# A batch's key-times-value product: from two products beside the running sums to one in an expert slot's bank, copied by ScalarE and masked by GpSimd

## The chip, the cores and the metric

The kernel runs on one NeuronCore of a Trainium2 chip. The metric is the device time of one execution in microseconds, lower is better. The profiled execution is one run with the hardware profiler on; its span goes from the first to the last instruction.

## The reference

Two layers over x of 16 batches of 256 tokens of 128 channels (4096 tokens). All of it is float32.

```
xn = layernorm(x)
x  = x + attn0(xn) + moe(xn)          # causal linear attention, 16 heads of 8; top 2 of 8 experts
xn = layernorm(x)
x  = x + attn1(xn) + channel_mix(xn)  # linear attention over 512 tokens; gated square of relu
```

attn0 is the part at issue. Keys and queries are rotated and put through elu + 1; then, for each batch and head,

```
KV_t    = sum of k_s (x) v_s for s <= t       # 8 x 8, running over the tokens
K_sum_t = sum of k_s for s <= t
y_t     = (q_t KV_t) / max(q_t K_sum_t, 1e-6)
```

The mixture of experts takes each token's two best of eight experts, with hidden = gelu(x W1 + b1), out = hidden W2 + b2, weighted by the two gates.

## The kernel before

**Tiles.** A tile is 128 tokens, a batch is two tiles. The experts' work is laid out in 71 slots of 128 rows, each with one expert. GpSimd gathers a slot's rows from a copy of xn in HBM by an indirect DMA (`gather`, L503), six slots ahead, into a ring of four buffers. TensorE transposes the rows (`xg_transpose`, L559), multiplies by W1 (`up`, L575), ScalarE copies and applies gelu (L596, L604), TensorE multiplies by W2 (`down`, L587), ScalarE copies the result out (L614) and SP stores it. From slot 17 on GpSimd also gathers experts' results back (`gather_y`, L520), five for six slots.

**Attention between the slots.** `steps` (L883) lays one tile of attention beside about every second slot: SUMS_AT is 1, 3, 5 and so on, 66 for the last. For tile i = 2b + r the vector engine multiplies keys by values (`attn_outer`, L685: 9 x 16 x 8 columns, the ninth of 9 being the keys themselves, put there by ScalarE at L671), ScalarE rounds that to a high part (L696), the vector engine takes the low part as a difference (L703; for tiles 1 to 12 GpSimd does a third of it, L716), and TensorE sums both over the tokens by a triangular matrix in three banks (`attn_cumsum`, L783 and L784). The vector engine multiplies the sums by the queries (`attn_apply`, L795) and reduces (L806); after the second tile come a reciprocal (L812), a division (L820) and phi (L656), which is elu + 1 for the batch after the next.

**What the first tile gives to the second.** Tile 1 of a batch also needs all of tile 0's sums. They come as a product of their own: K^T V of the first tile (`attn_KV`, L729, 128 columns, and L730, 16 columns of ones for the sum of keys), written by TensorE right ahead of the running sums of the batch before into the gap behind the first bank's 384 columns; the banks' windows therefore stand 520 columns apart (`NEXT`). The vector engine multiplies by the heads' mask into SBUF (`attn_mask_KV`, L735, tile KV0). Beside an expert slot TensorE then transposes the second tile's queries (L748, at slots QT_AT) and multiplies them by KV0 (L753, at slots REST_AT = SUMS_AT[2b]; batch 0 at slot 2), both written into columns 128 and up of the slot's own bank, between `up` and `down`; ScalarE copies them out ahead of the slot's result (`attn_beside_scalar`, L757 and L762).

**Order.** It is written out by hand. Each engine runs its own list in order and waits on semaphores. TensorE takes, in a step j: transpose of slot j+2, `up` of j+1, running sums if j is in SUMS_AT, what stands beside the slot, `down` of j. ScalarE takes copy of j+2, gelu of j+1, keys and high part in the step behind a sum, and the copies of slot j. A float32 product shows as two records in the trace.

**Gates.** The experts' gates are worked out by the vector engine ahead of the slots (`gates`, L1837 to L1843), and split in two parts (`split_gates`, L1849 and L1850); TensorE first needs them at the transposes of batch 0, in step 6.

## Time and profile before

| | |
|---|---|
| time, three runs | 348.57, 349.37, 349.54 us; median 349.37 us |
| profiled execution | 349.86 us, span 348.1 us |
| TensorE (PE) busy | 330.2 us, 95% |
| VectorE (DVE) busy | 318.9 us, 92% |
| ScalarE (ACT) busy | 278.4 us, 80% |
| GpSimd (POOL) busy | 225.3 us, 65% |
| granted TensorE clock | 0.995 of full |
| slots | 62 to 264 us of the span |

A row of the time line gives start, duration, engine, line, operation, tile written and tiles read, shape, and in brackets how long the engine had been idle before it and what ended that. A duration runs a little past the start of the next instruction, since instructions are pipelined, so that start to start is the pace. A wait for several semaphores is put down to the one that came last by the profile.

### The profile page before, as it was taken

To read this page: it belongs to the slowest core of one execution; us is meant where nothing else is said; L and a number is where in the kernel's file an instruction comes from. 1 tells how busy PE (TensorE), PEld (TensorE's weight loads), DVE (VectorE), ACT (ScalarE), POOL (GpSimd) and SP (SyncE) were. 2 spreads that over 40 slices of the span, in tenths; PEclk is the share of its full clock that TensorE was granted. 3 is DMA by queue.
4 is the path that set the end of the run, shared out by engine and by line. 5 is a ranking of instruction groups with operands and counts; after the bars stand their busy time and mean duration, and the time that the engine had idled before them with its cause. 6 is when DMAs were issued, how large, how long until landed. Compare 5 with 4: busy or idle time off the path is not lost.

```text
span 348.1 us, 9108 instructions
## 1 busy us (share of the span) xinstructions
PE 330.2 (95%) x2457; PEld 293.9 (84%) x2457; DVE 318.9 (92%) x590; ACT 278.4 (80%) x805; POOL 225.3 (65%) x238
## 2 busy tenths in 40 slices
PE   7999968889999999999999899999998999999995
PEld 3878424689999999999999899999997788778875
DVE  5899999989999999999899899999979799998665
ACT  2987956977899898889788778879997788777751
POOL 3799101876776688777777768777877278874110
PEclk9999989999999999999999999999999999999999
DMA  5785595334444555664655555676452002221012
GB/s 161 213 237 141 147 427 206 107 109 137 137 138 138 140 149 162 159 189 136 178 164 161 166 161 153 160 190 161 122 144 70 1 17 54 59 57 32 30 32 60
DMA packets 47120, 47.04 MB, mean 135 GB/s; under 512 B 8528, under 2 KB 35312, under 8 KB 46816
## 3 DMA queue, kind: packets, MB, share of 16 engines
q1 hardware_dynamic: 42032, 37.23, 35.4%
q0 software_dynamic: 4320, 8.86, 10.8%
q10 hardware_dynamic: 720, 0.38, 0.5%
q8 instruction: 22, 0.36, 0.4%
q14 instruction: 26, 0.21, 0.2%
HBM read 32.88 MB, written 13.50 MB: 133 GB/s over the span
## 4 chain that ended last, share of the span: by engine, by line
PE 78%; DVE 15%; DMA 2%; issue 2%; ACTq 1%; ACT 0%; SPq 0%; DVEq 0%
PE banks L575 17%; PE banks L587 17%; PE banks L783 5%; PE banks L784 5%; PE banks L1106 3%; PE banks L559 2%; PE banks L1182 2%; PE banks L1135 2%; PE banks L1164 2%; PE banks L1144 2%; PE banks L868 2%; PE banks L1116 2%; PE banks L1152 2%; DVE qk_exp L408 2%; PE banks L1171 2%
## 5 line engine op out<-in xcount | busy, mean ns | idle before, releaser
L503 POOL DMA_INDIRECT xg<-xn_rows,slot_tok x71 | 85.6, 1206 | 44.7 <-DVE slot_at L1819 23.0
L604 ACT ACTIVATE xT<-banks,b1T 128x128 f32<-128x128 f32 x284 | 81.8, 378 | 12.3 <-PE banks L575 11.9
L520 POOL DMA_INDIRECT qk_exp<-expert_rows,ranki x64 | 70.2, 1097 | 18.4 <-issue 17.1
L575 PE MATMUL banks<-xgT,w 128*128 128x128 f32 x568 | 75.5, 276 | 0.2 <-ACT xgT L596 0.2
L587 PE MATMUL banks<-w_sb,xT 128*128 x568 | 75.2, 275 | 0.1
L587 PEld LDWEIGHTS banks<-w_sb,xT 128*128 128x128 f32 x568 | 69.3, 192 | 0.9 <-issue 0.3
L575 PEld LDWEIGHTS banks<-xgT,w 128*128 128x128 f32 x568 | 69.0, 192 | 0.8 <-issue 0.7
L795 DVE TENSOR_TENSOR cq<-banks,phi 128x1152 f32<-128x1152 f32 x32 | 43.2, 1350 | 5.7 <-PE banks L784 5.7
L806 DVE TENSOR_REDUCE late<-cq 128x144 f32<-128x1152 f32 (+1 forms) x32 | 45.5, 1421 | 0.1
L696 ACT CAST high<-outer 128x1152 fp32r<-128x1152 f32 x32 | 37.0, 1156 | 6.8 <-DVE outer L685 5.0
L703 DVE TENSOR_TENSOR low<-outer,high 128x1152 fp32r<-128x1152 f32 (+1 forms) x32 | 38.7, 1210 | 1.5 <-ACT high L696 1.3
L685 DVE TENSOR_TENSOR outer<-phi,qkv 128x1024 f32<-128x1024 f32 x32 | 39.4, 1233 | 0.0
L783 PE MATMUL banks<-high,tri_r 128*128 128x384 f32 x96 | 34.8, 363 | 0.0
L784 PE MATMUL banks<-low,tri_r 128*128 128x384 f32 x96 | 32.2, 336 | 0.0
L335 PE MATMUL banks<-zeros_bf 128*128 128x512 bf16 x96 | 26.3, 415 | 1.0 <-DVE zeros_bf L1660 1.0
L321 ACT ACTIVATE xn_all<-x_sb,shift,rstd 128x128 f32<-128x128 f32 x60 | 24.9, 487 | 0.0
L1057 POOL TENSOR_TENSOR outer<-outer,x_sb 128x512 f32<-128x512 f32 x7 | 8.9, 1276 | 22.4 <-DVE outer L1052 22.3
L614 ACT COPY ye<-banks 128x128 f32<-128x128 f32 x71 | 19.9, 280 | 2.3 <-PE banks L587 2.3
L559 PE MATMUL banks<-cst,xg 128*128 128x128 f32 x71 | 19.6, 276 | 2.1 <-issue 1.9
L716 POOL TENSOR_TENSOR low<-outer,high 128x384 fp32r<-128x384 f32 x12 | 12.8, 1070 | 10.9 <-DVE phi L656 8.0
L596 ACT COPY xgT<-banks 128x128 f32<-128x128 f32 x71 | 19.6, 276 | 0.0
L303 POOL TENSOR_TENSOR rstd<-ve,mhalf 128x4 f32<-128x4 f32 x16 | 18.5, 1154 | 1.2
(224 smaller groups left out, 701.3 us busy)
## 6 DMA issues: line engine op xcount, KB each, us to landing
w<-in_L_ffn_W SPq DMA_DIRECT2D x71, 256.0 KB
expert_rows<-ye SPq DMA_DIRECT2D x71, 64.0 KB
expert_rows<-x_sb SPq DMA_DIRECT2D x2, 2048.0 KB, 9.8
x_sb<-in_L_attn_x SPq DMA_DIRECT2D x8, 256.0 KB, 4.5
xn_rows<-xn_all SPq DMA_DIRECT2D x8, 256.0 KB, 4.1
w_sb<-in_L_ffn_W SPq DMA_DIRECT2D x8, 256.0 KB, 4.5
out<-outer SPq DMA_DIRECT2D x7, 256.0 KB, 2.3
xg<-xn_rows,slot_tok POOLq DMA_INDIRECT x71
```

The lines of the kernel that those rows point to most:

```text
L503: pool.indirect_dma_start(out=xg[n][:, :], out_offset=None, in_=xn_dram, in_offset=bass.IndirectOffsetOnAxis(ap=slot_tok[:, j:j + 1], axis ...
L520: pool.indirect_dma_start(out=y_moe[:, i, k, :], out_offset=None, in_=y_dram, in_offset=bass.IndirectOffsetOnAxis(ap=ranki[:, 0, k, i:i + ...
L575: last = nc.tensor.matmul(slot_bank(j)[:, c * P:(c + 1) * P], w1[n][:, c * P:(c + 1) * P], xgT[p][:, :], start=True, stop=True)
L587: last = nc.tensor.matmul(y, hidT[p][:, c, :], w2_sb[:, ds(e * NC + c, 1), :], start=(c == 0), stop=(c == NC - 1))
L604: last = nc.scalar.activation(hidT[p][:, c, :], slot_bank(j)[:, c * P:(c + 1) * P], ACT.Gelu_apprx_tanh, bias=b1T[:, ds(e * NC + c, 1)])
L685: nc.vector.tensor_tensor(outer_of(r)[:, 0:DH, :, :], k.unsqueeze(1).broadcast_to([P, DH, H, DH]), vv.unsqueeze(3).broadcast_to([P, DH, H, ...
L696: nc.scalar.copy(high[kept(r, p)], outer[r]).then_inc(high_ready, 1)
L703: nc.vector.tensor_tensor(low[n][:, cols], outer[r][:, cols], high[n].bitcast(f32)[:, cols], ALU.subtract).then_inc(low_ready, 1)
L783: nc.tensor.matmul(o, tri_r[:, :], high[at][:, cols], start=True, stop=False)
L784: last = nc.tensor.matmul(o, tri_r[:, :], low[at][:, cols], start=False, stop=True)
L795: nc.vector.tensor_tensor(cq.rearrange("p (n e h d) -> p n e h d", n=NBANK, h=H, d=DK)[:, :, :, :, 0:DH], cum.rearrange("p n (e h d) -> p ...
L806: nc.vector.tensor_reduce(sums[:, r, :, :].rearrange("p h e -> p e h"), cq4[:, :, :, 0:DK if r else DH], AX.X, ALU.add).then_inc(sums_read ...
```

## The change

It does five things.

1. The product of keys and values is one matmul of 144 columns, its ones taken from sixteen columns behind the values (which held the router's logits), set to one by a GpSimd memset once the logits are read. It stands in `attn_beside`, in columns 368 to 511 of the slot's bank, at slots KV_AT = 0 for batch 0 and SUMS_AT[2b-2] + 1 for the others.
2. ScalarE copies it to KV0 in that slot's `attn_beside_scalar`; GpSimd multiplies KV0 by the mask in place, at the head of the next iteration of its loop over slots, ahead of a gather.
3. The running sums have no product ahead of them, don't wait for KV_ready, and their banks' windows stand 512 columns apart.
4. The vector engine no longer has the mask in its list.
5. Of the gates' operations the last three come after the first low part (`share_gates`), and `split_gates` comes after tile 0.

Some semaphores are merged, which moves no work. The diff, cut to its core:

```
-    def attn_KV(pe, b):
-        pe.wait_ge(phi_ready, b + 1)
-        k = phib[b % 2][:, 0, D:2 * D]
-        nc.tensor.matmul(first_sums[:, 0:D], k, qkv3[:, 2 * b, 2 * D:3 * D], start=True, stop=True)
-        nc.tensor.matmul(first_sums[:, D:DA], k, ones_r[:, 0:H].bitcast(f32), start=True, stop=True).then_inc(KV_ps, 1)
-    def attn_mask_KV(v, b):
-        v.wait_ge(KV_ps, b + 1)
-        nc.vector.tensor_tensor(KV0..., first_sums..., const("head_mask")..., ALU.mult).then_inc(KV_ready, 1)
+    def attn_mask_KV(pool, b):
+        pool.wait_ge(KV_raw, b + 1)
+        kv0 = KV0.rearrange("p (e h) -> p e h", h=H)
+        nc.gpsimd.tensor_tensor(kv0, kv0, const("head_mask")..., ALU.mult).then_inc(KV_ready, 1)
+    KV_AT = [0] + [SUMS_AT[2 * b - 2] + 1 for b in range(1, B)]
...
     def attn_beside(pe, j, bank):
+        if j in KV_AT:
+            b = KV_AT.index(j)
+            pe.wait_ge(phi_ready, b + 1)
+            if b == 0:
+                pe.wait_ge(pool_const, 5)
+            nc.tensor.matmul(bank[:, 4 * D - DA:4 * D], phib[b % 2][:, 0, D:2 * D], qkv3[:, 2 * b, 2 * D:2 * D + DA],
+                             start=True, stop=True)
...
     def attn_beside_scalar(act, j, bank):
+        if j in KV_AT:
+            nc.scalar.copy(KV0, bank[:, 4 * D - DA:4 * D]).then_inc(KV_raw, 1)
...
     def attn_cumsum(pe, b, r, p):
-        if i >= 1:
-            pe.wait_ge(KV_ready, 1 + i // 2)
-        if i == 0:
-            attn_KV(pe, 0)
-        if r == 1 and till(b, B - 2):
-            attn_KV(pe, b + 1)
-            o = ps_all[:, n * NEXT:n * NEXT + EB * D]
+            o = ps[n][:, 0:EB * D]
...
             for j in range(NS):
+                if j - 1 in KV_AT:
+                    attn_mask_KV(pool, KV_AT.index(j - 1))
                 if j + AHEAD < NS:
                     gather(pool, j + AHEAD)
...
             gates()
             attn_low(v, 0, 0, 0)
-            split_gates()
+            share_gates()
             attn_low(v, 0, 1, 0)
             for b in range(B):
                 for r in range(2):
                     tile(b, r, b % 2)
+                    if 2 * b + r == 0:
+                        split_gates()
```

The vector engine at the start of the slots, before, behind the outer products of batch 0 (sel and the first late are the gates, xn_all their split parts, w_in is KV0):

```order
L1841 TENSOR_TENSOR sel<-r 128x32
L1842 TENSOR_TENSOR sel<-r 128x32
L1843 TENSOR_TENSOR late<-late,sel 128x256
L703 TENSOR_TENSOR low<-outer,high 128x1152
L1849 CAST xn_all<-late 128x64x8
L1850 TENSOR_TENSOR xn_all<-late,xn_all 128x64x8
L703 TENSOR_TENSOR low<-outer,high 128x768
L795 TENSOR_TENSOR cq<-banks,phi 128x144x8
L685 TENSOR_TENSOR outer<-phi,qkv 128x1024
L735 TENSOR_TENSOR w_in<-banks,cst 128x144
L806 TENSOR_REDUCE late<-cq 128x9x16
```

The same place after:

```order
L703 TENSOR_TENSOR low<-outer,high 128x1152
L1841 TENSOR_TENSOR sel<-r 128x32
L1842 TENSOR_TENSOR sel<-r 128x32
L1843 TENSOR_TENSOR late<-late,sel 128x256
L703 TENSOR_TENSOR low<-outer,high 128x768
L790 TENSOR_TENSOR cq<-banks,phi 128x144x8
L685 TENSOR_TENSOR outer<-phi,qkv 128x1024
L801 TENSOR_REDUCE late<-cq 128x9x16
L703 TENSOR_TENSOR low<-outer,high 128x768
L1849 CAST xn_all<-late 128x64x8
L1850 TENSOR_TENSOR xn_all<-late,xn_all 128x64x8
L790 TENSOR_TENSOR cq<-banks,phi 128x144x8
```

Three gate operations moved behind the first low part, the two that split moved behind tile 0, and the mask is gone.

GpSimd around slot 23, in the stretch where it gathers both ways (xg is a gather of a slot's rows, qk_exp one of experts' results, low the third part of a low part), before:

```order
L716 TENSOR_TENSOR low2<-outer1,high2 128x384
L520 DMA qk_exp<-expert_rows,ranki 128x128
L503 DMA xg0<-xn_rows,slot_tok 128x128
L503 DMA xg1<-xn_rows,slot_tok 128x128
L716 TENSOR_TENSOR low0<-outer0,high0 128x384
L520 DMA qk_exp<-expert_rows,ranki 128x128
```

And after, where w_in is KV0 under the mask:

```order
L716 TENSOR_TENSOR low2<-outer1,high2 128x384
L520 DMA qk_exp<-expert_rows,ranki 128x128
L503 DMA xg0<-xn_rows,slot_tok 128x128
L727 TENSOR_TENSOR w_in<-w_in,cst 128x144
L503 DMA xg1<-xn_rows,slot_tok 128x128
L716 TENSOR_TENSOR low0<-outer0,high0 128x384
```

One operation of 144 columns came into GpSimd's list for each batch, ahead of a gather.

TensorE at the second tile of a batch, before: the output projection of an earlier batch (L868, L871), the two products, then the running sums and the transpose of the queries.

```order
L868 MATMUL banks<-wT,late 128x128 x2
L871 MATMUL banks<-bias,gT 128x256
L729 MATMUL banks<-qkv,phi 128x128
L730 MATMUL banks<-ones_r,phi 128x16
L783 MATMUL banks<-high,tri_r 128x384
```

After, the product stands one slot earlier, between that slot's `up` and `down`:

```order
L829 MATMUL banks<-cst,late 128x128 x2
L575 MATMUL banks<-xgT,w_3 128x128 x4
L1338 TENSOR_LOAD slot_exp
L742 MATMUL banks<-qkv,phi 128x144
L587 ISA
L587 MATMUL banks<-w_sb,xT 128x128
```

Two products ahead of the sums became one beside the slot before.

## Rows read from the trace of the kernel before

**Rows 1.** Busy us in two stretches: length, PE, PEld, DVE, ACT, POOL, clock, DMA
```profile
76.00:120.00 44.00, 44.00 (x367) 43.70 (x366) 40.97 (x46) 38.19 (x129) 29.28 (x23) 1.00 0.46 133
120.00:200.00 80.00, 78.45 (x655) 77.85 (x654) 76.87 (x93) 68.92 (x233) 64.12 (x58) 1.00 0.58 163
```
**Rows 2.** Time line of TensorE, start of the slots: start, duration, engine, line
```profile
67.91 1.12 PE L575 MATMUL banks<-xgT,w 128*128 128x128 f32 x8
...
69.63 0.49 PE L729 MATMUL banks<-qkv,phi 128*128 128x128 f32 x2 [0.60 <-DVE low L703]
...
71.25 1.05 PE L587 MATMUL banks<-w_sb,xT 128*128 x8
...
74.78 0.48 PE L753 MATMUL banks<-w_in 128*128 128x144 f32 x2 [1.48 <-ACT xT L604]
```
**Rows 3.** Time line of the vector engine, the same place
```profile
67.41 0.21 DVE L1841 TENSOR_TENSOR sel<-r 128x32 f32<-128x32 f32 x1
...
68.22 1.36 DVE L703 TENSOR_TENSOR low<-outer,high 128x1152 fp32r<-128x1152 f32 x1
69.49 0.42 DVE L1849 CAST xn_all<-late 128x512 fp32r<-128x512 f32 x1
...
70.56 0.95 DVE L703 TENSOR_TENSOR low<-outer,high 128x768 fp32r<-128x768 f32 x1
...
74.38 0.29 DVE L735 TENSOR_TENSOR w_in<-banks,cst 128x144 f32<-128x144 f32 x1
...
78.70 1.36 DVE L795 TENSOR_TENSOR cq<-banks,phi 128x1152 f32<-128x1152 f32 x1 [1.69 <-PE banks L784]
```
**Rows 4.** Time line of ScalarE, the same place
```profile
66.34 1.14 ACT L696 CAST high<-outer 128x1152 fp32r<-128x1152 f32 x1
...
69.59 0.25 ACT L757 COPY w_in<-banks 128x128 f32<-128x128 f32 x1
```
**Rows 5.** Time line of GpSimd, the same place
```profile
70.70 1.63 POOL L503 DMA_INDIRECT xg<-xn_rows,slot_tok  x1 [0.30 <-issue]
```
**Rows 6.** Time line of TensorE around one batch's product
```profile
133.83 0.39 PE L729 MATMUL banks<-qkv,phi 128*128 128x128 f32 x2
...
134.20 0.42 PE L783 MATMUL banks<-high,tri_r 128*128 128x384 f32 x1
...
140.27 0.41 PE L753 MATMUL banks<-w_in 128*128 128x144 f32 x2
140.52 1.05 PE L587 MATMUL banks<-w_sb,xT 128*128 x8
```
**Rows 7.** GpSimd's element-wise lines: count, ns min/median/max, first and last start
```profile
L716 POOL TENSOR_TENSOR low<-outer,high x12: 1002/1015/1384, 72.4 to 137.5; 128x384 fp32r<-128x384 f32 x12
L307 POOL TENSOR_TENSOR minus<-mv,rstd x15: 200/201/388, 8.5 to 320.5; 128x4 f32<-128x4 f32 x15
```
**Rows 8.** Time line of GpSimd and the vector engine, an overlap
```profile
188.65 2.08 POOL L520 DMA_INDIRECT qk_exp<-expert_rows,ranki  x1 [0.30 <-issue]
...
188.56 1.35 DVE L703 TENSOR_TENSOR low<-outer,high 128x1152 fp32r<-128x1152 f32 x1
```
**Rows 9.** Time line of GpSimd, its one pause; its last slot gather; TensorE's last L753
```profile
201.22 1.96 POOL L503 DMA_INDIRECT xg<-xn_rows,slot_tok  x1 [1.10 <-PE banks L559]
...
250.33 0.96 POOL L503 DMA_INDIRECT xg<-xn_rows,slot_tok  x1 [0.30 <-issue]
...
254.61 0.41 PE L753 MATMUL banks<-w_in 128*128 128x144 f32 x2
```
**Rows 10.** phi on the vector engine; `down` of the slot of KV_AT on TensorE, two batches
```profile
84.45 0.68 DVE L656 SCALAR_TENSOR_TENSOR phi<-qk_exp,qkv 128x512 f32<-128x512 f32 x1
...
85.91 1.06 PE L587 MATMUL banks<-w_sb,xT 128*128 x8
...
153.45 0.69 DVE L656 SCALAR_TENSOR_TENSOR phi<-qk_exp,qkv 128x512 f32<-128x512 f32 x1
...
154.00 1.06 PE L587 MATMUL banks<-w_sb,xT 128*128 x8
```

More of the change, by code:

```diff
@@ L415, in split_biases @@
         pool.wait_ge(bias_in, 16 * 5)
-        nc.gpsimd.tensor_copy(bias_part[:, 0, :].bitcast(f32r), bias_sp[:, :]).then_inc(bias_split, 1)
-        pool.wait_ge(bias_split, 1)
+        nc.gpsimd.tensor_copy(bias_part[:, 0, :].bitcast(f32r), bias_sp[:, :]).then_inc(bias_step, 1)
+        pool.wait_ge(bias_step, 1)
         nc.gpsimd.tensor_tensor(bias_part[:, 1, :].bitcast(f32r), bias_sp[:, :], bias_part[:, 0, :], ALU.subtract
-                                ).then_inc(bias_split, 1)
+                                ).then_inc(bias_step, 1)
     def place_biases(act):
         act.wait_ge(bias_rows, 16 * 18)
-        nc.scalar.copy(bias[:, :], bias_raw).then_inc(bias_ready, 1)
+        nc.scalar.copy(bias[:, :], bias_raw).then_inc(bias_step, 1)
     def rope_terms(g, f):
@@ L720, in build @@
     THIRD, LOW_SHARED = 2 * EB * D, 12
[L721 to L736 removed]
+    def attn_mask_KV(pool, b):
+        pool.wait_ge(KV_raw, b + 1)
+        kv0 = KV0.rearrange("p (e h) -> p e h", h=H)
+        nc.gpsimd.tensor_tensor(kv0, kv0, const("head_mask")[:, P:P + H].unsqueeze(1).broadcast_to([P, E9, H]), ALU.mult
                                 ).then_inc(KV_ready, 1)
     QT_AT = [0] + [SUMS_AT[2 * b - 1] for b in range(1, B)]
+    KV_AT = [0] + [SUMS_AT[2 * b - 2] + 1 for b in range(1, B)]
     REST_AT = [SUMS_AT[0] + 1] + [SUMS_AT[2 * b] for b in range(1, B)]
     def attn_beside(pe, j, bank):
+        if j in KV_AT:
[5 more added lines that the diff above has]
+                             start=True, stop=True)
         if j in QT_AT:
@@ L865, in attn_project @@
         if b == 0:
-            pe.wait_ge(bias_ready, 1)
+            pe.wait_ge(bias_step, 3)
         for t in range(2):
@@ L1027, in mask_KV @@
     def mask_KV(v, g):
-        v.wait_ge(KV_ps, B + g + 1)
+        v.wait_ge(KV_ps, g + 1)
         if from_(g, 1):
@@ L1396, in _ @@
                     sp.wait_ge(zeros_ready, 2)
-                    sp.wait_ge(bias_split, 2)
+                    sp.wait_ge(bias_step, 2)
                     spread_biases(0, 2)
@@ L1562, in _ @@
             pool.wait_ge(logits_read, 1)
+            nc.gpsimd.memset(qkv3[:, 0:NT:2, 3 * D:NW], 1.0).then_inc(pool_const, 1)
             for n in range(NB):
@@ L1840, in gates, with share_gates @@
                 done(nc.vector.reciprocal(row(3), row(9)))
+            def share_gates():
                 TT(sel[0][:, :], row(8), row(3), ALU.mult)
@@ L1858, in tile @@
                     attn_outer(v, b + 1, r, 1 - p)
-                if i == 0:
-                    attn_mask_KV(v, 0)
-                if r == 1 and till(b, B - 2):
-                    attn_mask_KV(v, b + 1)
                 attn_sums(v, i, r)
```

20 lines of the change are left out of this document (8 added, 12 removed).

## The prediction, made before the run

> **What bounds the kernel now.** I read the busy times by stretch first. While the slots run, TensorE is the full engine: 44.00 of 44 us between 76 and 120, 78.45 of 80 between 120 and 200. The vector engine has 40.97 and 76.87 there, so behind 120 it is nearly as full. GpSimd has 29.28 of 44 and then 64.12 of 80 [rows 1]; that second number hides that each indirect DMA is followed by 0.30 us of issue that isn't counted as busy. Next I read GpSimd's time line over the slots: from 120 us to its last slot gather it goes from one operation straight to the next and pauses for a release longer than a few tenths once, 1.10 us at 201.22 [rows 9]. So there are three engines to watch: TensorE sets the pace, the vector engine is close, and GpSimd, at 65% of the span, has no room in the second half of the slots. Last comes the start of the slots, the one place where TensorE waits for something this change touches.
>
> **The change, part by part.**
>
> *The start.* Before, TensorE ends `up` of slot 2 at 67.91 + 0.89 = 68.80, waits 0.60 for the low part of tile 0, does the two products and the sums (69.63 to 71.25), `down` of slot 1, transposes, `up` of slot 3, then waits 1.48 before L753 at 74.78 [rows 2]. That wait is put down to a gelu, but L753 needs KV0, and the mask on the vector engine runs from 74.38 to 74.67 [rows 3]: the mask ended it. It came so late since the list has gates, low part, split, low part, apply and outer ahead of it.
> After: batch 0's product stands ahead of `down` of slot 0; a float32 product of 144 columns takes 140.52 - 140.27 = 0.25 [rows 6], so `up` of slot 2 ends at 69.05. The low part of tile 0 no longer has share_gates ahead (68.22 - 67.41 = 0.81 [rows 3]) and ScalarE's high part has ended at 67.48 [rows 4], so it runs from about 67.5 to 68.8: no wait. The sums cost 71.25 - 70.10 = 1.15, where 70.10 is 69.63 plus the two products' 0.47. Then `down` 0.89, transpose 0.11, `up` 0.89, product of batch 1 0.25: 69.05 + 3.29 = 72.34 for L753. Is KV0 there? ScalarE's copy starts about where L757 did, 69.59, and costs about its 0.25 [rows 4]; GpSimd is free at 70.40, ahead of the gather at 70.70 [rows 5], and masks until about 70.9. Yes. Gain: 74.78 - 72.34 = 2.4 us.
> The vector engine must follow. Its apply of tile 1 stood at 78.70 after 1.69 of idleness [rows 3]; it loses the mask (0.29) ahead of that and gets the split (70.56 - 69.49 = 1.07) in the same stretch instead of ahead of the second low part. I get its next applies about 2 us earlier, which is enough, as the sums that wait for it come two slots later.
>
> *The products on TensorE.* Before, from L729 to the first sum 134.20 - 133.83 = 0.37 a batch; after, 0.25 [rows 6]. Batch 1's new 0.25 is counted above, so it saves all its 0.37; batches 2 to 15 save 0.12 each, 14 x 0.12 = 1.7. TensorE's own gain is thus 2.4 + 0.4 + 1.7 = 4.5 us. At slot 18, where GpSimd's full stretch begins, it is 2.4 + 0.4 + 3 x 0.12 = 3.2.
>
> *The copy on ScalarE.* 0.25 x 16, behind the high part and ahead of the slot's result. ScalarE has 68.92 of 80 [rows 1], and the result is needed three slots later: nothing.
>
> *The mask on GpSimd.* No row has 144 columns. Four columns take 0.20, 384 take 1.00 [rows 7]; the line through them gives 0.50. Bounds: 0.20 from below, and from above 0.50 plus a whole operation of the vector engine. For the rows show that the two block each other: a gather that began 0.09 behind a low part took 2.08 where one alone takes 0.96 [rows 9], the low part's 1.35 longer less a little [rows 8]. The usual case is the short one (L716, which reads SBUF like the mask, has a median of 1.015 and a maximum of 1.384), so I take c = 0.55 a mask. The memset of ones lies in the time in which GpSimd waits to begin its gathers: nothing.
> Ahead of slot 18 GpSimd has a third of its time free [rows 1], which covers five masks (b = 0 to 4). Behind it nothing is free but the 1.10, and each mask pushes all that follows. What is late first? A slot's gather is issued six slots ahead of its use, but KV0 only three or four, so KV0 is due first: the mask of batch 15 stands ahead of the gather at 250.33 and its L753 is at 254.61 [rows 9]. GpSimd's list is free for that mask at 250.03; its start moves 3.2 earlier with TensorE, the pause of 1.10 goes, ten masks (b = 5 to 14) come in ahead: 250.03 - 3.2 - 1.1 + 10 x 0.55 = 251.2, masked at 251.7, L753 at 251.8. That is **2.8 us** ahead of 254.61, less than TensorE's own 4.5: GpSimd sets it. In general the gain at that point is 8.3 - 10 c. Behind it the lengths stay as they are.
>
> *The new wait for phi.* Before, the product stood behind a whole further `up`; now it stands at `down` of the slot before and holds that `down`, the next transpose and all of TensorE up while phi isn't there. Before, phi of batch 2 ended at 85.13 and that `down` began at 85.91, 0.78 to spare; for batch 8 phi ended at 154.14 and `down` began at 154.00, so it would have been held 0.14 [rows 10]. So TensorE can no longer run ahead of the vector engine there. The vector engine gets 0.29 a batch back, over twice TensorE's 0.12, and this holds as long as GpSimd's mask doesn't block it. With my 2.8 TensorE falls back anyway, so I add nothing.
>
> *A rule against this change.* Rows 8 show one order of the pair. The Trainium skill (SBUF - State Buffer, "Who interferes with whom") says that a VectorE instruction with two inputs in SBUF and a GpSimd instruction that reads SBUF exclude each other for their whole length, whichever issues second waiting. By that rule the mask can also hold an outer product or a low part for up to its 0.50; the rows agree for one direction. It is the second rival below.
>
> **The sum.** 349.86 (profiled) - 2.8 = 347.1; the median of the runs is 0.49 below the profiled one, so 346.6.
>
> **The rivals.**
> *A, GpSimd hides the masks:* c near 0.35, or its list has more give than its time line shows. Then TensorE's 4.5 comes through, less 0.1 of waits for phi: 4.4, median 345.0. The 1.55 us that TensorE idles between 120 and 200 [rows 1] could go too, since a freer vector engine ends them: down to 343.5. For it: gathers are issued six slots ahead. Against: the sum above.
> *B, the two block each other:* each mask catches a low or outer in flight or holds one for its 0.50 a batch. The vector engine then gets 0.29 back and gives 0.50; at 96% busy, with phi now in TensorE's way, it loses 0.21 x 10 = 2.1 and the phi waits of some 0.1 to 0.2 come each batch: 3.2 - 2.1 - 1.1 = 0, median 349.4.
> *C, slower, GpSimd's mask costs much more:* behind a low part of 1.35 on average half of it, 0.50 + 0.45 and more, c = 0.95. Gain 8.3 - 9.5 = -1.2: TensorE stands at L753 for KV0 in most batches from slot 40 on; median 350.6. It turns from gain to loss at c = 0.83.
> *D, the order isn't what I read* (KV0 late at the start too, since GpSimd's gather ahead of it is long): the start's 1.48 stays; gain about 1.3, median 348.1.
>
> **Chances.** My forecast 0.42, A 0.24, B 0.12, C 0.12, D 0.10. What a measurement of this kernel can tell from no change is 0.3%, 1.05 us. Faster by more: forecast and A whole, half of D, less the forecast's own tail towards c = 0.72: 0.68. Same: B, the rest of D and that tail: 0.19. Slower: C and a little of B: 0.13. The range takes in A without the idle time's end and stops short of C: 344.2 to 349.8.
>
> **What would show it.** Start: L753 of batch 0 at 72 to 72.6 with no wait ahead, and the first sum at 69.1. GpSimd: the mask's median near 0.50, hardly any pause from 120 to the last gather, and waits of TensorE at L753 late in the slots whose releaser is the mask; if there are none, A. Vector engine: waits of TensorE at the new product for phi, a few tenths, and more idle ahead of apply. I am wrong if TensorE waits at the new product by more than half a us a batch, if the mask takes over 0.8, or if L753 of batch 0 is behind 73.

## The result: 1% slower, where 0.8% faster was forecast

| | before | after |
|---|---|---|
| time, median of six runs each | 349.06 us (348.47 to 350.19) | 352.40 us (351.71 to 353.83) |
| profiled execution | 349.86 us, span 348.1 us | 351.71 us, span 349.1 us |
| slot 2's transpose | 65.56 us | 64.42 us |
| slot 21's, behind slot 2's | 55.33 us | 55.59 us |

The ratio after to before is 1.0091, 95% interval 1.0073 to 1.0109: slower by more than the 0.3% that can be told from no change. The time is outside the range given (344.2 to 349.8). Ratios here and below leave out runs that took over 1.5% longer than the fastest of their kernel.

The two spans differ by 1.0 us only, since in the profiled execution after the slots began 1.1 us earlier (slot 2's transpose stands anywhere from 64.4 to 67.1 us in the traces of this case), and that execution is the fastest of its six. So I compare below by lead: the time from slot 2's transpose (L559) to that of a later slot. After minus before it is -3.0 us at slot 6, -1.4 at slot 9, -0.95 at 13, -0.4 at 17, +0.3 at 21, +1.7 at 29, +0.3 at 65, and +2.2 at slot 70. There is a gain at the start as forecast, then two losses: an **early** one, 4.7 us between slots 6 and 29, of which 1.5 come back by slot 65, and a **late** one of 2 us in the last five slots.

The page of after, busy times and then the chain of work that ended last (shares of the span), with two groups of the costliest instructions (count, busy us, mean ns, idle before them and its releaser):

```profile
PE 328.8 (94%) x2425; PEld 290.9 (83%) x2425; DVE 321.2 (92%) x574; ACT 279.6 (80%) x821; POOL 234.9 (67%) x255
...
PE 42%; DVE 29%; POOL 15%; issue 8%; DMA 3%; ACT 1%; ACTq 1%; DVEq 0%; SPq 0%; POOLq 0%
...
L696 ACT CAST high<-outer 128x1152 fp32r<-128x1152 f32 x32 | 36.9, 1154 | 10.9 <-DVE outer L685 9.6
...
L685 DVE TENSOR_TENSOR outer<-phi,qkv 128x1024 f32<-128x1024 f32 x32 | 43.7, 1369 | 0.0
```

The same lines of before:

```profile
PE 78%; DVE 15%; DMA 2%; issue 2%; ACTq 1%; ACT 0%; SPq 0%; DVEq 0%
...
L696 ACT CAST high<-outer 128x1152 fp32r<-128x1152 f32 x32 | 37.0, 1156 | 6.8 <-DVE outer L685 5.0
...
L685 DVE TENSOR_TENSOR outer<-phi,qkv 128x1024 f32<-128x1024 f32 x32 | 39.4, 1233 | 0.0
```

TensorE's share of the chain fell from 78% to 42%; the vector engine's rose from 15% to 29%, and GpSimd, which before isn't in the chain, has 15%. The vector engine lost its mask, about 0.3 us sixteen times, and is busy 2.3 us longer all the same: its outer products take 4.3 us more in sum, and ScalarE waits for them 9.6 us instead of 5.0. The two stretches of [rows 1] read now:

```profile
76.00:120.00 44.00, 42.30 (x338) 40.66 (x337) 43.69 (x44) 37.57 (x130) 32.08 (x27) 1.00 0.49 138
120.00:200.00 80.00, 77.55 (x638) 76.16 (x637) 77.47 (x86) 68.38 (x236) 65.76 (x62) 1.00 0.56 158
```

Between 76 and 120 us TensorE fell from 44.00 to 42.30 busy and the vector engine rose from 40.97 to 43.69 of 44: the bound has moved to the vector engine, in the very stretch in which GpSimd has a quarter of its time free.

**The early loss in the rows.** Before, L716 (GpSimd's third of a low part) runs beside the apply, and the outer product that follows takes its plain length:

```profile
90.06 1.36 DVE L795 TENSOR_TENSOR cq<-banks,phi 128x1152 f32<-128x1152 f32 x1 [0.31 <-PE banks L784]
90.20 1.01 POOL L716 TENSOR_TENSOR low<-outer,high 128x384 fp32r<-128x384 f32 x1 [0.57 <-PE banks L784]
91.34 1.22 DVE L685 TENSOR_TENSOR outer<-phi,qkv 128x1024 f32<-128x1024 f32 x1
```

GpSimd and the vector engine at the same place, around slot 10, after:

```profile
86.50 0.96 DVE L703 TENSOR_TENSOR low<-outer,high 128x768 fp32r<-128x768 f32 x1
86.73 1.09 POOL L727 TENSOR_TENSOR w_in<-w_in,cst 128x144 f32<-128x144 f32 x1 [0.61 <-ACT w_in L756]
87.38 1.35 DVE L790 TENSOR_TENSOR cq<-banks,phi 128x1152 f32<-128x1152 f32 x1
87.96 0.99 POOL L503 DMA_INDIRECT xg<-xn_rows,slot_tok  x1
88.65 2.42 DVE L685 TENSOR_TENSOR outer<-phi,qkv 128x1024 f32<-128x1024 f32 x1
88.97 1.01 POOL L716 TENSOR_TENSOR low<-outer,high 128x384 fp32r<-128x384 f32 x1
```

The mask first waits 0.61 us for ScalarE's copy, a wait that the kernel before doesn't have; then it takes 1.09, since a low part of the vector engine (L703) is under way. Gather and L716 stand behind it, and L716 lands on the outer product: L716 runs its 1.01 to 89.98, and the outer product, begun at 88.65, ends 1.09 behind that. It takes 2.42 instead of 1.22 though it began ahead of L716. Four outer products of after take 2.4 us, at 70.78, 88.65, 100.57 and 112.49; none of before does. The mask's own line:

```profile
L727 POOL TENSOR_TENSOR w_in<-w_in,cst x16: 488/670/1572, 68.8 to 254.9; 128x144 f32<-128x144 f32 x16
```

Min, median and max are 0.49, 0.67 and 1.57 us; the first six take 1.16, 1.09, 1.09, 1.08, 1.09 and 1.57, the last ten 0.62 on average, all sixteen 0.83.

Behind 112.49 no outer product is long, yet 1.5 of the 4.7 us are lost behind slot 21. There TensorE waits for L716 itself, which GpSimd's list, now without a pause and with a mask of 1.57 at 124.41, brings about 2 us later against slot 2's transpose than before:

```profile
127.14 1.00 POOL L716 TENSOR_TENSOR low<-outer,high 128x384 fp32r<-128x384 f32 x1
...
128.20 0.44 PE L778 MATMUL banks<-high,tri_r 128*128 128x384 f32 x1 [0.81 <-POOL low L716]
...
140.15 0.45 PE L778 MATMUL banks<-high,tri_r 128*128 128x384 f32 x1 [0.50 <-POOL low L716]
```

Before, TensorE never waits for L716.

**The late loss in the rows.** Where the slots end, GpSimd has the first layer-2 normalizations in its list (L301 to L309: shifts that ScalarE needs for layer 2's xn, L321). Time line of after:

```profile
246.71 1.06 POOL L303 TENSOR_TENSOR rstd<-ve,mhalf 128x4 f32<-128x4 f32 x1
...
249.29 0.20 POOL L309 TENSOR_TENSOR shift<-zero,minus 128x4 f32<-128x4 f32 x1
...
249.53 0.88 ACT L321 ACTIVATE xn_all<-x_sb,shift,rstd 128x128 f32<-128x128 f32 x2 [1.77 <-POOL shift L309]
...
251.00 0.30 PE L559 MATMUL banks<-cst,xg 128*128 128x128 f32 x1 [1.46 <-issue]
```

ScalarE waits 1.77 us for GpSimd's shift, with a slot's copies queued behind that on ScalarE, and TensorE stands 1.46 ahead of the next transpose. In before the shift of the same batch came at 243.6, ScalarE ran L321 at 248.93 without a wait, and TensorE didn't stand there. GpSimd is 5.6 us later with it.

```profile
243.64 1.19 POOL L309 TENSOR_TENSOR shift<-zero,minus 128x4 f32<-128x4 f32 x1
...
248.93 0.87 ACT L321 ACTIVATE xn_all<-x_sb,shift,rstd 128x128 f32<-128x128 f32 x2
```

Slot 67 loses 1.2 us by this. The next two transposes of after, at 253.45 and 257.06, wait 0.21 and 0.17 for their own gathers, which before no transpose there does, so the gathers themselves had become nearly too late as well.

### The profile page after: what moved, and what is told of

It is laid out like the page before. It is cut to its first block, busy times and chain, and to the rows that moved or that the text cites. A ratio compares the mean times of both kernels' runs of the same rounds, so it can differ in the third digit from the quotient of the medians.

```text
span 349.1 us, 9047 instructions
## 1 busy us (share of the span) xinstructions
PE 328.8 (94%) x2425; PEld 290.9 (83%) x2425; DVE 321.2 (92%) x574; ACT 279.6 (80%) x821; POOL 234.9 (67%) x255
## 4 chain that ended last, share of the span: by engine, by line
PE 42%; DVE 29%; POOL 15%; issue 8%; DMA 3%; ACT 1%; ACTq 1%; DVEq 0%; SPq 0%; POOLq 0%
PE banks L587 7%; PE banks L575 6%; POOL xg L503 6%; POOL qk_exp L520 6%; DVE outer L685 5%; DVE late L801 4%; PE banks L1101 3%; DVE cq L790 2%; PE banks L1177 2%; PE banks L1130 2%; PE banks L1159 2%; PE banks L1139 2%; DVE low L703 2%; PE banks L1111 2%; PE banks L1147 2%
## 5 line engine op out<-in xcount | busy, mean ns | idle before, releaser
L503 POOL DMA_INDIRECT xg<-xn_rows,slot_tok x71 | 83.3, 1173 | 39.3 <-DVE slot_at L1817 21.8
L790 DVE TENSOR_TENSOR cq<-banks,phi 128x1152 f32<-128x1152 f32 x32 | 43.2, 1349 | 2.9 <-PE banks L779 2.8
L685 DVE TENSOR_TENSOR outer<-phi,qkv 128x1024 f32<-128x1024 f32 x32 | 43.7, 1369 | 0.0
L703 DVE TENSOR_TENSOR low<-outer,high 128x1152 fp32r<-128x1152 f32 (+1 forms) x32 | 38.7, 1209 | 4.3 <-ACT high L696 4.3
L778 PE MATMUL banks<-high,tri_r 128*128 128x384 f32 x96 | 34.1, 355 | 1.3 <-POOL low L716 1.3
L321 ACT ACTIVATE xn_all<-x_sb,shift,rstd 128x128 f32<-128x128 f32 x60 | 24.9, 485 | 1.9 <-POOL shift L309 1.8
L335 PE MATMUL banks<-zeros_bf 128*128 128x512 bf16 x96 | 24.9, 399 | 1.0 <-DVE zeros_bf L1658 1.0
L559 PE MATMUL banks<-cst,xg 128*128 128x128 f32 x71 | 19.9, 280 | 4.1 <-issue 3.4
L778 PEld LDWEIGHTS banks<-high,tri_r 128*128 128x128 f32 x96 | 18.2, 189 | 1.9 <-POOL low L716 1.9
```

The lines of the kernel that those rows point to most:

```text
L503: pool.indirect_dma_start(out=xg[n][:, :], out_offset=None, in_=xn_dram, in_offset=bass.IndirectOffsetOnAxis(ap=slot_tok[:, j:j + 1], axis ...
L685: nc.vector.tensor_tensor(outer_of(r)[:, 0:DH, :, :], k.unsqueeze(1).broadcast_to([P, DH, H, DH]), vv.unsqueeze(3).broadcast_to([P, DH, H, ...
L703: nc.vector.tensor_tensor(low[n][:, cols], outer[r][:, cols], high[n].bitcast(f32)[:, cols], ALU.subtract).then_inc(low_ready, 1)
L778: nc.tensor.matmul(o, tri_r[:, :], high[at][:, cols], start=True, stop=False)
L790: nc.vector.tensor_tensor(cq.rearrange("p (n e h d) -> p n e h d", n=NBANK, h=H, d=DK)[:, :, :, :, 0:DH], cum.rearrange("p n (e h d) -> p ...
```

## Theories

*Order (my theory of the early loss):* not the amount of GpSimd's work counts but its place. The mask waits for the copy and stands ahead of a gather and L716, which pushes L716 under the outer product of an engine without slack.

*Amount (rival):* GpSimd's additional work, or its contention with the vector engine at whatever place, costs the time; or the change of the products costs it (the wait for phi, say), with the mask only near.

*Backlog (theory of the late loss):* behind slot 18 GpSimd's list is full, so each mask makes everything behind it later, up to layer 2's shifts. By the rows above it also has the part of the early loss behind slot 21.

All experiments ran on other chips than the comparison above. There the kernel before takes 384 to 388 us, and every kernel stands for long in the second half of the slots, its releaser given as "remote", which means that the profile doesn't tell what ended the wait. Here the changed kernel itself (us in total, times, longest):

```profile
DVE cq L790 <- remote: 23.7, 5, 13.2
...
ACT xT L604 <- remote: 18.1, 10, 5.7
```

The granted clock falls there too. Each of these traces has 10 to 20 us at half clock (1.2 GHz) somewhere between 265 and 305 us, after TensorE had idled (in change_again it waited 2.06 us up to 279.88, and the clock is at half from 280.6); in the traces of the comparison above it is 1.00 there. The changed kernel again (length, PE, PEld, DVE, ACT, POOL, clock, DMA):

```profile
270.00:300.00 30.00, 22.18 (x128) 20.29 (x126) 15.41 (x32) 14.32 (x48) 15.93 (x18) 0.77 0.27 70
```

So of these runs two things are used: the ratio to the kernel before on the same chip, and the lead to slot 21 (about 120 us), which lies ahead of that disturbance: the changed kernel gave 55.56 us there and 55.59 in the undisturbed trace. The first "remote" wait of over 0.7 us in any of them ends at 129.9 us. One thing spoils the lead by up to 0.6 us: in best_again, late_once, late_double and best_third slot 2's transpose itself waited 0.7 to 1.3 us for its gather, which makes their leads look short (53.13 or 53.14; best_mix, the same kernel as best_again and best_third, has 53.72 without that wait).

## Experiments: where the early loss comes from

**mask_vector**: the new product and copy, the mask on the vector engine.

```
-        nc.gpsimd.tensor_tensor(kv0, kv0, head_mask..., ALU.mult)
+        nc.vector.tensor_tensor(kv0, kv0, head_mask..., ALU.mult)
...
                 attn_apply(v, b, r, p)
+                if i == 0:
+                    attn_mask_KV(v, 0)
+                if r == 1 and till(b, B - 2):
+                    attn_mask_KV(v, b + 1)
```

> The change with the mask alone taken off GpSimd: the vector engine multiplies KV0 in place, between apply and outer product of the batch's second tile; ScalarE's copy, the one product in the slot's bank and the order of the gates stay. Theory 1 (GpSimd's mask costs all of it: it pushes the third of the low part at L716 into the outer product's start, so that every batch up to slot 29 loses about 0.9 us on the vector engine, 4.7 us in all, and its backlog holds TensorE some 2 us near slot 67): both losses go, and the gain of about 3 us at the start stays. About 345.5 to 347 us, ratio to before 0.988 to 0.994; outer products back at a mean of 1.23 us. Rival 2 (the product's new place, with its wait for phi, holds TensorE): still at least 350, with TensorE waiting at the product. Rival 3 (ScalarE's extra copy delays the high parts): still about 350.

Ratio 0.9936 (0.9887 to 0.9985), lead to slot 21 53.39 us. As expected, the early loss is gone, so new product, copy and wait for phi don't make it. Here batch 0's product with KV0 waits a little for the mask:

```profile
72.29 0.36 DVE L727 TENSOR_TENSOR w_in<-w_in,cst 128x144 f32<-128x144 f32 x1
...
72.71 0.51 PE L752 MATMUL banks<-w_in 128*128 128x144 f32 x2 [0.73 <-issue]
```

**no_mask**: the changed kernel without the mask.

```
-            nc.scalar.copy(KV0, bank[:, 4 * D - DA:4 * D]).then_inc(KV_raw, 1)
+            nc.scalar.copy(KV0, bank[:, 4 * D - DA:4 * D]).then_inc(KV_ready, 1)
-                if j - 1 in KV_AT:
-                    attn_mask_KV(pool, KV_AT.index(j - 1))
```

> The change without any mask: ScalarE's copy of the product is used as it is, so that the rest of the first tile mixes all heads (a part of the computation left out); nothing stands in its place on any engine. Theory 1: a little below the kernel with the mask on the vector engine, by up to 15 x 0.3 us if that engine bounds the slots and by nothing if TensorE does: 344.5 to 346.5 us. Rival 2 or 3 (place of the product, or copy): 350 or more, as neither is touched.

Ratio 0.992 (0.9871 to 0.9969), lead 53.65. No outer product ahead of slot 21 is long. So the mask on GpSimd costs 55.56 - 53.65 = 1.9 us up to slot 21, and without any mask the kernel is no faster than with the mask on the vector engine: there it costs nothing that can be measured.

**mask_behind**: the mask on GpSimd, behind L716 instead of ahead of the gather.

```
             for j in range(NS):
-                if j - 1 in KV_AT:
-                    attn_mask_KV(pool, KV_AT.index(j - 1))
                 if j + AHEAD < NS:
                     gather(pool, j + AHEAD)
                 if j in SUMS_AT[0:LOW_SHARED]:
                     ...
+                if j - 1 in KV_AT:
+                    attn_mask_KV(pool, KV_AT.index(j - 1))
```

> The change with GpSimd's mask behind the gather and behind the third of the low part in the same iteration, ahead of both before. As much GpSimd work as in the change, in another order. Theory 1, first half (the collision of L716 with the outer product is a matter of order: the mask waits for ScalarE's copy and holds L716 back into the outer product's start): the 4.7 us lost up to slot 29 go, outer products fall from a mean of 1.37 to about 1.25 us; the late loss near slot 67, about 2 us, stays, since the backlog is as long: about 347 to 348.5 us. If instead the amount of GpSimd's work does it, whatever its order: 350 to 352.

Ratio 0.9986 (0.9944 to 1.0027), lead 53.12, the shortest but one of all, with the same work on GpSimd. And that although batch 0's mask comes later here and TensorE waits 0.61 us for it at L752. Its time line at the same place:

```profile
88.21 1.35 DVE L790 TENSOR_TENSOR cq<-banks,phi 128x1152 f32<-128x1152 f32 x1
88.43 1.00 POOL L716 TENSOR_TENSOR low<-outer,high 128x384 fp32r<-128x384 f32 x1 [0.22 <-issue]
89.39 0.49 POOL L727 TENSOR_TENSOR w_in<-w_in,cst 128x144 f32<-128x144 f32 x1
89.48 1.49 DVE L685 TENSOR_TENSOR outer<-phi,qkv 128x1024 f32<-128x1024 f32 x1
```

L716 runs beside the vector engine's apply (L790), which reads the banks of sums and isn't slowed by it; the mask takes its plain 0.49, and holds the outer product up by 0.27 only. TensorE doesn't wait for L716 either. Up to slot 21 order is right for the early loss, and amount falls. The ratio is worse than mask_vector's though the lead is better, which points at something later, the late masks; but the two intervals overlap.

**before_idle_op**: the kernel before, with an additional GpSimd operation of the mask's form on a tile that nobody reads.

```
+            AT = [1] + [SUMS_AT[2 * b - 2] + 2 for b in range(1, B)]
...
+                if j in AT:
+                    nc.gpsimd.tensor_tensor(it, it, head_mask..., ALU.mult).then_inc(idle_done, 1)
                 if j + AHEAD < NS:
                     gather(pool, j + AHEAD)
```

> The kernel before with one more GpSimd operation a batch, 144 columns multiplied by the mask in a tile that nobody reads, at the place in GpSimd's list where the change has its mask, with no wait for another engine. Nothing else of the change. Theory 1: the late loss comes (2 us near slot 67), since GpSimd has no room from slot 18 on; the early loss comes only in part, as the operation doesn't wait for ScalarE and so needn't push L716 into the outer product: 350.5 to 353 us, ratio 1.004 to 1.012. If GpSimd has more give than that, or if the early loss needs the other parts of the change: 349, no difference.

The time, 386.08 us in four runs against 384.06, has no interval and decides nothing: the late loss that I expected here is neither seen nor excluded. The lead is 55.86 (55.33 in before), and there is no outer product over 2 us. The operation stands at the mask's place in the list, but waits for no other engine:

```profile
86.42 1.22 DVE L687 TENSOR_TENSOR outer<-phi,qkv 128x1024 f32<-128x1024 f32 x1
...
88.49 0.50 POOL L1579 TENSOR_TENSOR idle_tile<-idle_tile,cst 128x144 f32<-128x144 f32 x1
...
90.74 1.01 POOL L718 TENSOR_TENSOR low<-outer,high 128x384 fp32r<-128x384 f32 x1
91.44 1.41 DVE L687 TENSOR_TENSOR outer<-phi,qkv 128x1024 f32<-128x1024 f32 x1
```

It takes 0.50, and L716's work (L718 here) overlaps the outer product only at its end: 1.41, not 2.42. For the collision place alone isn't enough; the phase in which the wait for the copy puts GpSimd counts too. For TensorE's wait for L716 it is enough: 0.64 us at 129.5 here. The changed kernel and early_only below have 0.79 and 0.80 at 128.5 and 128.8, and no kernel whose early masks stand behind L716, on the vector engine, or nowhere has any. So this part of the early loss needs only an additional operation ahead of L716.

**mask_next**: meant to test just that. The masks of batches 1 to 5 ahead of a gather again, one turn of GpSimd's loop later, when the copy is long done and that turn has no L716; those of batches 6 to 15 on the vector engine.

```
+                if j - 2 in KV_AT and KV_AT.index(j - 2) in range(1, 6):
+                    attn_mask_KV(pool, KV_AT.index(j - 2))
                 if j + AHEAD < NS:
                     gather(pool, j + AHEAD)
```

> As the mixed placement, but GpSimd takes the masks of batches 1 to 5 in front of a gather again, only one turn of its loop later than the change does (by then ScalarE's copy is long done, and that turn holds no third of a low part). Theory, the wait for the copy and the place right ahead of gather and L716 push L716 under the outer product: no outer product over 2 us among the first ten, lead from the transpose of slot 2 to that of slot 21 at 53.1 to 53.8. Rival, any mask on GpSimd in front of a gather costs it (the length of the operation, not its place): lead of 55.0 to 55.6 and three or more outer products over 2 us.

Ratio 0.9916 (0.9876 to 0.9957), lead 53.70. There is one outer product over 2 us, where none was expected, behind the mask of batch 0, which I had left in its place:

```profile
69.74 1.16 POOL L727 TENSOR_TENSOR w_in<-w_in,cst 128x144 f32<-128x144 f32 x1 [0.19 <-issue]
...
71.73 2.43 DVE L685 TENSOR_TENSOR outer<-phi,qkv 128x1024 f32<-128x1024 f32 x1
72.05 1.01 POOL L716 TENSOR_TENSOR low<-outer,high 128x384 fp32r<-128x384 f32 x1
...
76.47 1.06 POOL L716 TENSOR_TENSOR low<-outer,high 128x384 fp32r<-128x384 f32 x1 [0.22 <-issue]
77.49 0.94 POOL L727 TENSOR_TENSOR w_in<-w_in,cst 128x144 f32<-128x144 f32 x1
...
79.27 1.21 DVE L685 TENSOR_TENSOR outer<-phi,qkv 128x1024 f32<-128x1024 f32 x1
```

With mask, gather and L716 in this order the outer product takes 2.43, with L716 ahead of the mask 1.21, in one kernel. But the rows also show that this experiment tells less apart than I meant: the turn before is the one that holds L716, so one turn later the mask again stands right behind L716, as in mask_behind. It confirms the order; how much of the push comes from the 0.6 us of waiting and how much from the mask's own 1.09 stays open.

## Experiments: the early and the late masks apart

**change_again**, the changed kernel as it is, as their base; **early_only**, masks of batches 0 to 5 on GpSimd as in the change, the others on the vector engine; **late_only**, the reverse; **best_mix**, batch 0 on GpSimd as in the change, 1 to 5 behind L716, the others on the vector engine. The edit of early_only, the others alike:

```
-                if j - 1 in KV_AT:
+                if j - 1 in KV_AT and KV_AT.index(j - 1) in range(6):
                     attn_mask_KV(pool, KV_AT.index(j - 1))
...
                 attn_apply(v, b, r, p)
+                if r == 1 and till(b, B - 2) and b + 1 in range(6, 16):
+                    attn_mask_KV(v, b + 1)
```

> The changed kernel itself, so that it shares its chip with the three below. Ratio to before 1.005 to 1.012 where the first comparison gave 1.0091. With the early loss (a transposes' lead of about 3 us over before at slot 6 turned into a lag of about 1.5 us at slot 29) and the late one (2 us at slots 66 to 69).

> GpSimd masks batches 0 to 5 as in the change, ahead of the gather; the vector engine masks batches 6 to 15 in place, between apply and outer product. Theory: the early loss stays (outer products of 2.42 us once a batch up to slot 26), the late one goes, since GpSimd's list is as long as before from slot 23 on. About 2 us less than the change: ratio to before 1.000 to 1.005. If the late loss was chance, as much as the change.

> The other half: the vector engine masks batches 0 to 5, GpSimd 6 to 15 ahead of the gather as in the change. Theory: no outer product of 2.42 us up to slot 26 and the lead of the start kept to slot 29, then GpSimd's backlog: it must take the late loss, and more of it, since TensorE comes some 4 us earlier and GpSimd can't follow. Ratio to before 0.992 to 1.000. If GpSimd's backlog costs nothing: the same as with the mask on the vector engine throughout.

> Meant to beat both: GpSimd masks batch 0 ahead of the gather and batches 1 to 5 behind the third of the low part, where it had time to spare; the vector engine masks batches 6 to 15, where GpSimd has none. Theory: the lead of 3 us at the start kept or grown to slot 29, no late loss. Ratio to before 0.985 to 0.993. If the collision isn't a matter of order on GpSimd, the lead is gone by slot 29 as in the change.

| kernel | ratio to before, 95% | lead to slot 21 |
|---|---|---|
| change_again | 1.0056 (1.0019 to 1.0094) | 55.56 |
| early_only | 0.9975 (0.9927 to 1.0023) | 55.60 |
| late_only | 0.9971 (0.9933 to 1.0009) | 53.43 |
| best_mix | 0.9896 (0.9842 to 0.9949) | 53.72 |

The lead follows the early masks alone: 55.6 where they are as in the change, 53.4 to 53.7 where not. In the time, taking away the late masks gains 0.8% (change_again to early_only) or 0.75% (late_only to best_mix), and mending the early ones 0.85% or 0.8%. Three of the four ratios are in the ranges expected; early_only is a little better than its own (1.000 to 1.005). The two losses add up and are about equally large, some 3 us each on these chips. Each of the four steps taken by itself is only just clear of its noise, which I estimate at 0.6% from the intervals.

**best_again, late_once, late_double**: more of the suspected cause. late_once is the mixed placement with the masks of batches 6 to 15 back on GpSimd; late_double has an idle operation of the mask's form behind each.

```
                     attn_mask_KV(pool, KV_AT.index(j - 1))
+                    if j - 1 > KV_AT[5]:
+                        it = idle_tile...
+                        pool.wait_ge(idle_done, KV_AT.index(j - 1) - 5)
+                        nc.gpsimd.tensor_tensor(it, it, head_mask..., ALU.mult).then_inc(idle_done, 1)
```

> The mixed placement once more, on its own chip session, beside two variants of it: batch 0's mask on GpSimd in front of the gather, those of batches 1 to 5 on GpSimd behind its third of the low part, those of 6 to 15 on the vector engine, behind the apply of the batch before. Both theories of the early loss expect the lead from the transpose of slot 2 to that of slot 21 at 53.7 us again (55.3 before, 55.6 with the change as it stands). If the late loss is GpSimd's backlog, this kernel, which has none, gains at least 3 us on before: ratio 0.985 to 0.993. If GpSimd's backlog is harmless, late_once gives the same time as this one.

> The mixed placement with the masks of batches 6 to 15 on GpSimd, in front of the gather. Backlog theory: ten masks of about 0.5 us are pushed into a list that has no pause, layer 2's deviations behind it (L309) come 3 to 5 us later than in best_again, and the kernel is 1.5 to 3 us slower than best_again, ratio to before 0.992 to 0.998. Rival, the vector engine pays as much for ten masks of 0.3 us as TensorE pays for GpSimd's lateness: same time as best_again within 0.5 us.

> As late_once, with one more GpSimd operation of the mask's form (128x144, on a scratch tile that nobody reads) behind each of the masks of batches 6 to 15: ten times 0.5 us more in GpSimd's list, nothing more for any other engine to wait for directly. Backlog theory: another 3 to 5 us of lateness at GpSimd's end of the slots, the transposes' waits move into the slots themselves, and the kernel is 2.5 to 5 us slower than late_once. Rival, there is still give in GpSimd's list: under 1 us slower than late_once.

Ratios 0.9887 (0.9834 to 0.994), 1.0005 (0.9961 to 1.0049) and 1.0018 (0.9953 to 1.0083); medians of the seven, nine and five runs behind the ratios 380.2, 382.5 and 385.2 us. The first ten masks cost 1.2% by the ratios, whose intervals don't meet, which is more than the 1.5 to 3 us expected, and 2.3 us by the medians, which is not. For the second ten the ratio says 0.1% and the medians 2.7 us: whether they cost the expected 2.5 to 5 us stays open. GpSimd's lateness itself goes with the dose. Its last gather of a slot, in that order of the three kernels:

```profile
267.67 0.94 POOL L503 DMA_INDIRECT xg<-xn_rows,slot_tok  x1 [0.31 <-issue]
```
```profile
274.10 1.79 POOL L503 DMA_INDIRECT xg<-xn_rows,slot_tok  x1 [0.16 <-issue]
```
```profile
279.63 0.99 POOL L505 DMA_INDIRECT xg<-xn_rows,slot_tok  x1 [0.16 <-issue]
```

It comes 6.4 and another 5.5 us later, ten times 0.6; slot 21's transposes stand at 119.2, 119.3 and 120.2, so 1.1 of these 12 were there already. That this lateness then acts through L309 is seen in the undisturbed trace above and only there: late in the slots ScalarE doesn't wait for L309 in any run on these chips (its waits of 0.2 to 0.6 us for it all end ahead of 30 us, in layer 1), while the waits of the other kind add up to tens of us. So the experiments show that the late masks cost time, and not by which wait.

## Experiments: what the gain at the start is made of

**gates_only**: the kernel before, with the gates' operations moved as in the change.

```
+            def share_gates():
...
             attn_low(v, 0, 0, 0)
-            split_gates()
+            share_gates()
             attn_low(v, 0, 1, 0)
...
+                    if 2 * b + r == 0:
+                        split_gates()
```

> The kernel before with only the gates' operations moved: three of them behind the first low part, the two that split behind tile 0. If the gates' order makes the gain at the start, the first sum of tile 0 comes about 0.6 us earlier relative to slot 2's transpose, the second tile's product with KV0 (L753, 9.2 us behind that transpose in the kernel before) comes near 7.5 to 8, and the kernel gains 0.8 to 1.5 us. If the moved mask and product make it, L753 stays behind 8.5 and the time within 0.3 us of before.

Ratio 1.0025 (0.9961 to 1.0089). L753 stands at 74.10 - 65.03 = 9.07 us behind slot 2's transpose, 9.22 in before. The first product (L729) comes at +3.43 instead of +4.07, 0.6 earlier as expected, but that only makes the next wait longer (1.99 instead of 1.48), and its cause is what the prediction said, the mask (73.71 to 74.01) and not the gelu:

```profile
68.46 0.49 PE L729 MATMUL banks<-qkv,phi 128*128 128x128 f32 x2
...
73.71 0.30 DVE L735 TENSOR_TENSOR w_in<-banks,cst 128x144 f32<-128x144 f32 x1
74.10 0.48 PE L753 MATMUL banks<-w_in 128*128 128x144 f32 x2 [1.99 <-issue]
```

**best_old_gates**: the mixed placement with the gates' order of before. **best_third**: the mixed placement again, as its base.

```
-            share_gates()
+            split_gates()
             attn_low(v, 0, 1, 0)
...
-                    if 2 * b + r == 0:
-                        split_gates()
```

> The mixed placement with the gates' operations back in the order of the kernel before (all of them ahead of the first low part, the split ahead of the second low part). If the moved product and mask alone make the gain at the start, batch 0's product with KV0 stands 6.5 to 7.0 us behind slot 2's transpose as in the mixed placement. If the gates' order is needed too, as the prediction's step has it, the running sums of tile 0 wait again 0.4 to 0.8 us for the low part, that product stands at 7.2 to 7.9, and the kernel is 0.3 to 1 us slower than the mixed placement.

> The mixed placement once more, beside the two above as their base: lead to slot 21 of 53.1 to 53.8, ratio to before 0.985 to 0.993.

```profile
68.89 0.44 PE L778 MATMUL banks<-high,tri_r 128*128 128x384 f32 x1 [0.44 <-DVE low L703]
...
72.18 0.41 PE L752 MATMUL banks<-w_in 128*128 128x144 f32 x2
```

The sums wait 0.44 for the low part again, and L752 stands at 72.18 - 64.83 = 7.35 instead of 71.93 - 65.20 = 6.73 in best_mix. Both are as expected. But the lead to slot 21 is 53.00 against best_mix's 53.72 (best_third's 53.14 has the late slot 2 in it), and the ratio 0.9864 (0.9755 to 0.9972, four runs) against best_third's 0.9891 (0.9861 to 0.9921), where 0.3 to 1 us slower was expected. In these traces the gates' new order brings 0.6 us at L752, and by slot 21 it has cost 0.7; in the time the old order is if anything the better one.

**Where that goes.** In no_mask, which has no collision at all ahead of slot 21, the kernel is 3.0 us ahead of before at slot 6 and 1.1 at slot 9. Part of what is between is a wait for the division of batch 0 on the vector engine, here in after:

```profile
81.47 0.33 PE L827 MATMUL banks<-cst,xn_all 128*128 128x128 f32 x1 [0.35 <-DVE late L815]
```

(0.35 in no_mask too, and 0.29 for a copy of ScalarE just ahead of it.) TensorE arrives at the vector engine's results earlier than these are made.

## Why the prediction was wrong

**The start** was right on TensorE: L752 of batch 0 was forecast at 72.34 without a wait, 2.4 us gained, and it stands at 71.13 in a phase 1.14 earlier, 2.5 gained. The rows, which answer to [rows 2]:

```profile
67.84 0.44 PE L778 MATMUL banks<-high,tri_r 128*128 128x384 f32 x1
...
70.89 0.41 PE L742 MATMUL banks<-qkv,phi 128*128 128x144 f32 x2
71.13 0.41 PE L752 MATMUL banks<-w_in 128*128 128x144 f32 x2
```

The step "I get its next applies about 2 us earlier, which is enough" fell. Even where nothing collides (no_mask), almost two thirds of the 3 us are gone by slot 9; a gain at one place holds only as far as the next engine has it too. Rival D (KV0 late at the start) is out.

**The products** were right: L742 to L752 is 0.24 us, 0.25 forecast. From slot 9 to slot 21 no_mask is 0.6 us faster than before, where three batches at 0.12 gave 0.36.

**The copy** costs ScalarE 0.26 to 0.27 a batch and nothing by itself. That GpSimd would wait for it, on the gathers' engine, I had not put into the sum: 2.6 us in five waits, four of them of 0.6. I had asked who waits for the mask, and not for whom the mask waits and what stands behind it.

**The mask** is where the sum broke. Its plain length was right (0.50 from the line through two rows, 0.49 measured), its mean is 0.83 and not 0.55. But the size isn't what failed first. "Ahead of slot 18 GpSimd has a third of its time free, which covers five masks" did. In this stretch, up to slot 21, which I had at nothing, the masks cost 1.9 us (change against no_mask), and behind it, to slot 29, TensorE waits 1.3 us for L716. The rest of the 4.7 us lost from slot 6 to slot 29 is the gain at the start melting away, as it does without any mask. A share of free time says that an engine can take the work, not that the operations behind it keep their places, and here the place of L716 against the outer product is worth 1.2 us each time to the vector engine. mask_behind keeps work and engine and changes only the order.

**What is late first** behind slot 18 I had as KV0, at L752. TensorE never waited there. It waited first for L716, 0.81 us at 128.20 and 0.50 at 140.15, and at the end of the slots, by way of ScalarE, for layer 2's shifts, the last small operations in the same list, 5.6 us late. I had looked for the next user of the changed tile, and not down GpSimd's list to its end. So "GpSimd sets it" was right, with the wrong victim, as far as one trace shows.

**The wait for phi** added next to nothing, as forecast: 0.2 us, once.

**Rivals.** B, the two engines block each other, had the mechanism (0.12), at 349.4 with 0.50 a batch; in fact it is 1.2 us, because it isn't the mask that blocks but L716 behind it. C had the sign, but L752 as its place, and the size of c doesn't bear it out. All sixteen masks have a mean of 0.83, its break-even; the ten that its formula counts (batches 5 to 14) have 0.72, and 8.3 - 7.2 would still be a gain of 1.1 us. With 0.13 for slower in all, I gave too little to GpSimd's and the vector engine's full lists meeting.

**The rule of the Trainium skill** (SBUF - State Buffer, "Who interferes with whom") spoke against the change, and the runs agree with both of its directions: a mask issued under a low part takes 1.09 instead of 0.49, and an outer product issued under a mask 1.49 instead of 1.22 (mask_behind). The 2.42 doesn't follow from it alone, since that outer product began ahead of L716.

## What to carry to other kernels

Before an operation is put into another engine's list, follow that list to its end: what it will wait for, what stands behind it, and beside what on a full engine those will then run. A free share of a third doesn't cover 0.5 us if this moves a long operation under one of a full engine, or makes it late for the engine that waits for it; the same operation one place later in the list gave the early gain. And give late work to the engine whose list still has give: here the mask belongs behind L716 early and on the vector engine late, which is 1.0 to 1.1% faster than before in three comparisons (0.9896, 0.9887, 0.9891), all on chips with the disturbance; where before takes 349 us it wasn't run. The mask on the vector engine throughout (0.9936) can't be told from it in the time.

## What the runs showed of the hardware

- An operation of the vector engine can lose although it began first. The outer product at 88.65 was ahead of L716 at 88.97, and L716 took its plain 1.01, the outer product 2.42, ending 1.09 behind L716's end. It had begun under a gather (87.96 to 88.95) that L716 followed at once. In mask_vector an outer product that began 0.11 behind a gather, with no L716 behind that, took a plain 1.22. What decides between the two I can't tell from the rows.
- A gather that begins about 0.1 us behind an outer product takes 1.9 to 2.0 us instead of 0.95 (86.42 in before, 84.17 in after: 1.95), while one that begins 0.1 ahead takes 1.03 and the outer product its plain 1.22 (89.25 in mask_vector). So the gathers have no fixed price: it depends on their phase.
- The mask's form, two inputs of 128x144 on GpSimd, takes 0.49; four columns take 0.20 [rows 7] and 384 take 1.00.
